# Nine moved channel blocks: statistics written from other queues, constant products put into TensorE's waits, and early mean shares made unscaled

## The reference

```python
def _displace(x, offset):            # 48 offsets, 8 channels each
    off_px = offset * 64.0
    off_int = round(off_px); sub = off_px - off_int
    # each block of 8 channels is shifted by (dx, dy) = off_int, zeros shifted in,
    # then convolved (3x3, same) with exp(-((kx+sub_x)^2 + (ky+sub_y)^2) / 0.5), normalised
    ...
x = x + _displace(_gn(x), offset)    # _gn: group norm, 32 groups of 12 channels
xr = transpose(_gn(x), (0, 2, 3, 1)).reshape(-1, 384)
y = pad(xr, 512) @ hadamard(512) / sqrt(512)
x = x + y[:, :384]                   # back in (16, 384, 32, 32)
```

## Time and profile before

| | us |
|---|---|
| median of 3 runs | 261.75 (259.67 to 261.84) |
| the profiled execution, device time | 261.49 |
| its span in the trace | 259.5 |
| what lies outside the span | 1.99 |

### The profile page before, as it was taken

One profiled execution on the slowest core, in us unless ns is written; L12 is line 12 of the kernel. 1 busy time (PEld: TensorE's weight loads), 2 busy tenths in 40 slices (PEclk: granted clock), 3 DMA queues, 4 the chain that ended last, 5 costly groups with the idle time before them and its releaser, 6 DMA issues.

```text
span 259.5 us, 2305 instructions
## 1 busy us (share of the span) xinstructions
PE 143.3 (55%) x616; PEld 87.5 (34%) x616; DVE 197.5 (76%) x321; ACT 136.2 (52%) x217; POOL 44.7 (17%) x49
## 2 busy tenths in 40 slices
PE   0000000508507249867920696999999999988610
PEld 0000000408507249756920532443333333333200
DVE  0799999999972169845760336999999999999940
ACT  1000999779761046035500199997788878880000
POOL 0000000000000053211233784000404184000000
PEclk9999999955955558997985559999999999999975
DMA  5999999999999208999960567219999999998798
GB/s 158 420 408 411 407 411 285 370 412 406 412 283 244 65 2 237 248 301 315 283 154 18 145 216 250 99 81 327 356 334 417 399 419 368 390 405 348 285 407 341
DMA packets 24845, 76.78 MB, mean 296 GB/s; under 512 B 6576, under 2 KB 6832, under 8 KB 24544
## 3 DMA queue, kind: packets, MB, share of 16 engines
q1 hardware_dynamic: 18928, 67.07, 71.7%
q0 software_dynamic: 5072, 9.51, 11.6%
q10 hardware_dynamic: 832, 0.05, 0.2%
HBM read 67.07 MB, written 29.99 MB: 374 GB/s over the span
## 4 chain that ended last, share of the span: by engine, by line
DVE 38%; DMA 33%; PE 9%; ACT 5%; issue 5%; SPq 5%; POOLq 0%; DVEq 0%
DMA ring<-x_pad 27%; DVE ring L934 22%; DVE parts L271 10%; PE ps L573 4%; PE ps L554 4%; DMA blk<-x_pad 4%; ACT blk L518 3%; DVE blk L271 2%; ACT parts L526 2%; DMA stat_rows<-blk_stat 2%; PE ps L563 2%; SPq L301 1%; SPq L289 1%; DVE halfstat L799 1%; DMA stat<-stat_rows 1%
## 5 line engine op out<-in xcount | busy, mean ns | idle before, releaser
L934 DVE SCALAR_TENSOR_TENSOR ring<-ps,beta,ring 128x1024 f32<-128x1024 f32 x48 | 59.8, 1280 | 0.0
L635 PE MATMUL ps<-parts,had_sb 128*128 128x512 f16 x216 | 54.0, 384 | 8.1 <-DVE parts L271 5.8
L563 PE MATMUL ps<-geo_sb,blk 128*128 128x128 f32 x72 | 12.5, 336 | 59.0 <-DMA blk<-x_pad 45.4
L799 DVE BATCH_NORM_STATS2 halfstat<-ring 128x6 f32<-128x512 f32 x64 | 38.9, 674 | 1.8 <-DMA ring<-x_pad 1.8
L573 PE MATMUL ps<-parts 128*128 128x160 f32 (+2 forms) x180 | 33.0, 348 | 10.4 <-ACT parts L460 10.4
L283 POOL DMA_INDIRECT ring<-x_rows,row_at x24 | 30.2, 1257 | 46.3 <-DMA ring<-x_pad 39.9
L518 ACT ACTIVATE blk<-ring,gn 128x1024 f32<-128x1024 f32 x32 | 37.8, 1226 | 0.0
L271 DVE TENSOR_TENSOR parts<-blk,parts 128x1024 f16<-128x1024 f32 x27 | 32.9, 1219 | 6.0 <-ACT parts L526 6.0
L573 PEld LDWEIGHTS ps<-parts 128*128 128x128 f32 x180 | 31.5, 225 | 11.4 <-ACT parts L460 10.6
L635 PEld LDWEIGHTS ps<-parts,had_sb 128*128 128x128 f16 x216 | 20.1, 99 | 44.0 <-DVE parts L271 13.2
L645 PE MATMUL ps<-ring,first_w 128*128 128x512 f32 x64 | 32.0, 624 | 0.0
(11 more groups left out here) (117 smaller groups left out, 136.6 us busy)
## 6 DMA issues: line engine op xcount, KB each, us to landing
ring<-x_pad SPq DMA_DIRECT2D x20, 1536.0 KB, 15.3
out<-ring SPq DMA_DIRECT2D x13, 1536.0 KB, 7.4
blk<-x_pad SPq DMA_DIRECT2D x15, 512.0 KB, 17.2
out<-ring SPq DMA_DIRECT2D x9, 512.0 KB, 6.0
x_rows<-blk POOLq DMA_DIRECT2D x6, 512.0 KB, 6.6
other_a<-x_pad SPq DMA_DIRECT2D x2, 512.0 KB, 9.1
x_rows<-other_a POOLq DMA_DIRECT2D x2, 512.0 KB, 6.5
geo_sb<-geo SPq DMA_DIRECT2D x1, 683.0 KB, 4.7
```

The lines of the kernel that those rows point to most:

```text
L563: last = pe.transpose(pixels[:, j // 4, 128 * (j % 4):128 * (j % 4 + 1)], shifted[:, 128 * j:128 * (j + 1)], eye)
L635: last = pe.matmul(ps[n % 4][:, h, :], had_sb[:, sign, :], part_of(n, t, part)[:, 512 * h:512 * (h + 1)], start=False, stop=ends and part ...
L799: last = dve.bn_stats(halfstat[:, i % 4, t, h, :], ring[:, t, place_of(i), 512 * h:512 * (h + 1)])
L934: dve.scalar_tensor_tensor(ring[:, m, place_of(i), :], ps[n % 4][:, :, :].rearrange("p a n -> p (a n)"), beta[:, i % BATCH:i % BATCH + 1], ...
```

## The change

- **Statistics of the blocks.** POOL no longer writes them. ACT does (`put_stat`), into a semaphore of its own, `stat_put`: blocks 0 to 3 inside its loop over the blocks, 4 to 8 behind its last mask. `blk_stat` has a slot for each block, so no buffer waits for the write. `blk_out` counts the write of the block only, 16. The read back of all statistics goes from POOL's queue to SP's, behind a wait for the nine writes.
- **Fetches of `blk_gn`.** SP issues those of blocks 0, 1, 3, 4 (before: 0, 1), ACT that of block 2 alone (before: 2, 3, 4).
- **Constant products.** `turn_over(n)` issues n products of the identity with 512 constant columns, into a PSUM half that nobody reads: 12 behind the early convolutions, 6 between the group sums and the first transposes of the block stage, 6 behind the last convolution.
- **Mean shares.** POOL makes the outer products of the unscaled `share`: block 0's as soon as DVE has made them (at image 8), block 1's behind ACT's last sum. To free `other_a` for this, ACT's two passes both write `aside[1]`, and the second waits for the first. When `blk_gn` is there, DVE works out one number for each block (`slope`, 128 x 1) and the addition is a SCALAR_TENSOR_TENSOR that scales the share.
- **DVE's order** at the start of the block stage: both partials, both additions, then mask 2, `finish(0)`, mask 3, `finish(1)`.

```diff
@@ sync
             def fetch_plain(k):
                 if k >= WIDE:
-                    sp.wait_ge(blk_out[k % WIDE], 32 * (k // WIDE))
+                    sp.wait_ge(blk_stat_done, k - WIDE + 1)
+                    sp.wait_ge(blk_out[k % WIDE], 16 * (k // WIDE))
...
-            for k in range(EARLY):
+            for k in (0, 1, 3, 4):
                 fetch_gn(sp, k)
...
+            sp.wait_ge(stat_put, 16 * FAST)
+            with sp.If(active > FAST):
+                sp.wait_ge(more_out, 32 * (OFFSETS - FAST))
+            sp.dma_start(stat[:, :, :, :].rearrange("p t b k -> p t (b k)"),
+                         stat_rows.rearrange("(t c) n -> c t n", t=CT)).then_inc(stat_patched, 16)
@@ gpsimd
             def leave(k, u):
-                c_at = pool.value_load(place[0:1, k, 0:1], min_val=0, max_val=CHANNELS - BIND)
                 pool.wait_ge(x1_done, k + 1)
                 pool.dma_start(x1_rows[...], own_x[u]).then_inc(blk_out[u], 16)
-                pool.wait_ge(blk_stat_done, k + 1)
-                pool.dma_start(stat_rows[...], blk_stat[:, u, :]).then_inc(blk_out[u], 16)
...
-                pool.wait_ge(slope_ready, k + 1)
+                pool.wait_ge(shares_made, 1)
+                if k == 1:
+                    pool.wait_ge(sum_stat_done, BATCH)
...
-            pool.dma_start(stat[...], stat_rows...).then_inc(stat_patched, 16)
@@ scalar
-                act.activation(aside[0], image, ACT.Identity, ..., accum_out=sums[:, 0, i:i + 1])
+                act.activation(aside[1], image, ACT.Identity, ..., accum_out=sums[:, 0, i:i + 1]).then_inc(sum_done_first, 1)
+                act.wait_ge(sum_done_first, i + 1)
...
-            for k in range(EARLY, DEEP + EARLY):
-                fetch_gn(act, k)
+            fetch_gn(act, EARLY)
+            def put_stat(k):
+                at = act.value_load(place[0:1, k, 0:1], min_val=0, max_val=CHANNELS - BIND)
+                act.wait_ge(blk_stat_done, k + 1)
+                act.dma_start(stat_rows[ds(at, BIND), :]..., blk_stat[:, k, :]).then_inc(stat_put, 16)
...
+                if k >= DEEP + EARLY:
+                    put_stat(k - DEEP - EARLY)
             mask_upper(FAST - 1)
+            for k in range(FAST - DEEP - EARLY, FAST):
+                put_stat(k)
@@ tensor
+            def turn_over(count):
+                for _ in range(count):
+                    pe.matmul(ps[1][:, 1, :], eye, geo_sb[:, G_SUM:G_SUM + 512], start=True, stop=True)
...
+            turn_over(12)
             group_sums(1, 0, lambda b: stat[:, b, :, 0])
             group_sums(2, 1, lambda b: moment[:, b, 1, :])
+            turn_over(6)
             pe.wait_ge(gn_done, 1)
...
+            turn_over(TURNS)
             group_sums(3, 0, ...)
@@ vector
             for k in range(EARLY):
                 dve.wait_ge(gn_in[k], 16)
-                dve.tensor_scalar(share[:, k, 0, :], share[:, k, 0, :], blk_gn[:, k, 0:1], blk_gn[:, k, 1:2],
-                                  ALU.mult, ALU.mult).then_inc(slope_ready, 1)
+                link(dve.tensor_tensor(slope[:, k:k + 1], blk_gn[:, k, 0:1], blk_gn[:, k, 1:2], ALU.mult))
                 partial(k).then_inc(partial_done, 1)
-            mask_block(EARLY)
             for k in range(EARLY):
                 dve.wait_ge(mean_share, k + 1)
                 dve.wait_ge(partial_done, k + 1)
-                dve.tensor_tensor(blk[:, k, :], blk[:, k, :], aside[k], ALU.add).then_inc(x1_done, 1)
+                dve.scalar_tensor_tensor(blk[:, k, :], aside[k], slope[:, k:k + 1], blk[:, k, :], ALU.mult, ALU.add).then_inc(x1_done, 1)
+            for k in range(EARLY):
+                mask_block(EARLY + k)
                 finish(k)
-                if k == 0:
-                    mask_block(EARLY + 1)
```

More of the change, by code:

```diff
@@ L32 @@
 EARLY_AT = 8
+TURNS = 6
 EARLY_FLIP = 10
@@ L158, in build @@
         blk_gn = sb("blk_gn", [128, FAST, 2])
+        slope = sb("slope", [128, EARLY])
         blk_half = sb("blk_half", [128, WIDE, 2, 6])
-        blk_stat = sb("blk_stat", [128, WIDE, 2])
+        blk_stat = sb("blk_stat", [128, FAST, 2])
         early = parts[:, :, :, :].rearrange("p a b c -> p (a b c)").bitcast(FP32)
@@ L209, in build @@
         centred = sem("centred")
-        slope_ready = sem("slope_ready")
+        shares_made = sem("shares_made")
         mean_share = sem("mean_share")
+        sum_done_first = sem("sum_done_first")
         partial_done = sem("partial_done")
@@ L233, in build @@
         stat_out = sem("stat_out")
+        stat_put = sem("stat_put")
         more_link = sem("more_link")
@@ L274, in fast_blocks_out @@
             for u in range(WIDE):
-                eng.wait_ge(blk_out[u], 32 * blocks_in(u))
+                eng.wait_ge(blk_out[u], 16 * blocks_in(u))
         def gather_part(eng, n, limit, signal):
@@ L347, in _ @@
                 for u in range(WIDE):
-                    sp.wait_ge(blk_out[u], 32 * blocks_in(u))
+                    sp.wait_ge(blk_out[u], 16 * blocks_in(u))
+                sp.wait_ge(stat_put, 16 * FAST)
                 with sp.Fori(FAST, OFFSETS) as k:
@@ L413, in _ @@
             pool.wait_ge(place_done, 1)
-            pool.wait_ge(stat_out, 16)
             for k in range(FAST):
@@ L449, in _ @@
                 act.activation(pivot[:, i:i + 1], image[:, 0:1], ACT.Copy)
-                act.activation(aside[0], image, ACT.Identity,
-                               bias=image[:, 0:1], scale=-1.0, accum_out=sums[:, 0, i:i + 1])
+                act.activation(aside[1], image, ACT.Identity,
+                               bias=image[:, 0:1], scale=-1.0, accum_out=sums[:, 0, i:i + 1]).then_inc(sum_done_first, 1)
+                act.wait_ge(sum_done_first, i + 1)
                 act.activation(aside[1], image, ACT.Square,
@@ L489, in _ @@
                     mask_upper(k - 1)
+                if k == DEEP + EARLY - 1:
+                    act.wait_ge(stat_out, 16)
+                if k >= DEEP + EARLY:
+                    put_stat(k - DEEP - EARLY)
             mask_upper(FAST - 1)
+            for k in range(FAST - DEEP - EARLY, FAST):
+                put_stat(k)
             active = act.value_load(count_i[0:1, 0:1], min_val=0, max_val=OFFSETS)
@@ L796, in _ @@
                     early_shares()
+                    dve.memset(scrap[:, 0:1], 0.0).then_inc(shares_made, 1)
                 for t in range(CT - 1):
@@ L884, in _ @@
                 dve.wait_ge(convolved, FAST)
+                dve.wait_ge(stat_put, 16 * FAST)
                 for u in range(WIDE):
-                    dve.wait_ge(blk_out[u], 32 * blocks_in(u))
+                    dve.wait_ge(blk_out[u], 16 * blocks_in(u))
                 with dve.Fori(FAST, OFFSETS) as k:
```

7 lines of the change are left out of this document (3 added, 4 removed).

## The result

| | before | after |
|---|---|---|
| median of 20 runs each | 262.56 (259.67 to 264.96) | 259.59 (256.45 to 262.11) |
| the profiled execution, device time | 261.49 | 259.88 |
| its span | 259.5 | 258.1 |

The ratio of after to before, run beside each other, is 0.986 with an interval of 0.983 to 0.989. That is 1.4% or 3.7 us faster. The ratio is taken over the fast runs of both kernels alone, those within 1.5% of the fastest, so it differs a little from that of the two medians, which are 3.0 us apart. The forecast was 254.1, in a range of 251.0 to 258.2. The sign is right, the gain is half of the 7.4 us forecast, and the time lies outside the range.

The account below looks back on a forecast made before the run. Bounds: DVE in the main stage; before it, slow-clock group sums with DVE's small steps, SP's DMA issue order, and the statistics' way. -5.0 (term 1 included) and -2.4 give -7.4 on 261.49: 254.1, range 251.0 to 258.2.

Parts of the forecast that it names:

- term 2: Block stage up to the last addition: earlier SP issues, shifted 7 at 102.6, last addition 5.0 us earlier, Term 1 included.
- about 105: Block stage: shifted 7's issue if two slow SP address loads come ahead and transposes stay slow, -3.3 us.
- rival (a): Block stage: DMA engines are the bound, earlier issues only land later; -3.9 us in all, 257.6; chance 0.20.
- The bound of the engines: Block stage: sixteen transfers at 296 GB/s take 28.3 us, through at 124.5, about when plain 8 lands at 124.8.
- Term 1: Group sums at the load stage's end: constant products keep the clock fast, second sum ends at 84.45 instead of 85.95, -1.5 us.
- My bound of -3.2: Group sums: the best case, if DVE isn't held and the clock is fast in both sums, -3.2 us.
- Term 3: Last block's statistics out and back: ACT writes, SP reads back, 5.5 us instead of 7.94, -2.4 us.
- Rival (c): After the last mask: ACT's last five issues are late through slow address loads, statistics' way +1.6 us, 258.1; chance 0.06.
- rival (d): Group sums: twelve constant products at the slow clock hold the first sum, +12.5 us; +6.6 in all, 268.1; chance 0.04.
- the cap by the gather: Main stage start: first gather lands at 139.9, doesn't bind, but caps further gain from the gn at 1.1 us.

Follow-up runs that it names:

- the kernel with `TURNS = 10` and late loads: Kernel after with SP's loads ahead, later POOL product, exchanged writes, block writes on ACT, ACT's loads before the `gn_rows` write, ten closing constant products: 0.977 against before.
- the later product: Kernel after with POOL's product for block 1 also waiting until DVE has handed over the sums (`sum_in`): 0.984 against before.
- the kernel with all edits together: Kernel after with SP's loads ahead, later POOL product, exchanged `gn_rows`/`stat_rows` writes, block writes on ACT, ACT's loads before the `gn_rows` write: 0.980 against before.
- the last kernel: Kernel after with SP's loads ahead, later product, exchanged writes, ACT's block writes, ACT's loads before its variance wait, ten closing constant products: 0.960 against before, median 251.27.
- the exchanged writes: Kernel after with SP's loads ahead, later POOL product, `gn_rows` written from ACT's queue and `stat_rows` from SP's: 0.971 against before, median 254.16.
- the last but one: Kernel after with SP's loads ahead, later product, exchanged writes, ACT's block writes, ACT's loads before its variance wait, six closing constant products: 0.961 against before, median 251.50.

## Why the forecast had the sign right and the size wrong

**The step that failed: term 2.** "Then one DMA each 1.3 us: ... shifted 7 at 102.6" and with it "-5.0 for the last addition". The trace gave +0.4, so the time gained came from terms 1 and 3 alone. What failed is that SP's issues were costed at 1.3 us each with every address load at its usual 0.28 us. I had seen one load of 1.91 us and allowed for two ahead of shifted 7 at the most, as a bound; two of them are 3.3 us, which from 102.6 gives 105.9 and not the "about 105" of that bound. There came three before it and two behind it, 7.4 us in all. The row I cited gave minimum, median and maximum of one line; the single loads of all three lines would have shown 4.5 us of excess before the change already. The rest of the working adds up: 102.6, and 1.0 for the first fetch (89.12 where I had 88.1), and 4.9 for the three slow loads ahead of shifted 7 make 108.5, and it went at 108.36. With the loads ahead of the stage it goes at 102.22, and the last addition comes 2.7 us earlier. But even then it begins at 129.06 and not 126.4. Landings had grown from 8.9 to 12.9 us, as rival (a) would have it. The bound of the engines that I had worked out "with no room to spare" from 296 GB/s allowed a last addition at 124.9, or 125.9 with the first fetch 1.0 us later than forecast, so at 295 GB/s it is not that bound which put it at 129.06. Only with the block writes on ACT's queue is the bound reached: 123.07 at 311 GB/s, with the first fetch 0.6 us earlier than forecast. So rival (a) is half right for a kernel whose SP keeps pace, and for the kernel after it isn't: its landings did not grow (8.9 us), and it lost the term to SP's loads.

That the block writes from POOL's queue slow the loads is shown by moving them to ACT: 7.4 to 2.3 us. What makes up the 2.3 us that remain, and by what path these writes act on SP, stays open.

**Term 1, -1.5 forecast, -0.5 measured.** The hold of DVE's TENSOR_SCALAR came as forecast from the one held row, 1.86 us for 0.17. The size is off in the second sum: forecast 1.6, measured 2.74. The hold that I counted as hidden behind the constant products ended 0.99 us after them, since they took 0.87 each and not 0.94. Over all kernels with twelve constant products the second sum goes with the idle time ahead of the first: without any it took 1.76, 1.78, 1.95, 2.06 and 2.29 us, with 0.99 it took 2.72, and with 1.8 to 2.5 it took 3.17, three times. One doesn't fit: the kernel with `TURNS = 10` and late loads had 0.46 us of idle time and 3.17. So the tendency is shown, a fixed relation isn't. By ratio the constant products are worth 0.7% or 1.8 us, which is near the 1.5 us of the term, though the term also holds the loss by POOL's product. My bound of -3.2 "if DVE isn't held and the clock is fast in both sums" is nearly what the later product gave: `gn` 2.5 us earlier than before, 84.6 for 87.1.

BN_STATS beside POOL's other product, for which I had taken 0, lost next to nothing. The product ran at 55.38 to 57.29, and DVE's four halves of an image took 2.47 us from 55.21 to 57.68, 2.42 elsewhere. Here the trace agrees with the Trainium skill (SBUF — State Buffer, "Who interferes with whom"), which says that a DVE instruction with at most one SBUF input, outside the two-port modes, does not contend with GpSimd. The held TENSOR_SCALAR of 1.86 us agrees with the same section, which counts tensor_scalar among the operations that can enter such a mode. It read SBUF; another TENSOR_SCALAR, which reads PSUM, took its usual 0.21 us beside POOL's product (at 80.02, product from 78.36 to 80.27, in the kernel with all edits together). Whether a TENSOR_TENSOR would be held too no run here shows: DVE's began when the product ended.

**Term 3, -2.4 forecast, -1.8 measured.** The statistics' write landed after 3.84 us, at the upper end of what I had allowed ("between 2.2 and 4.0"); a block write issued at 133.36 was still under way. The read back took 1.97 instead of 2.3. By ratio the statistics' part is worth 2.8 us, give or take 1. If more than the 1.8 is in it, that may lie in the plain fetches that wait for one write less; no run separates that.

**The rest.** Rival (c), ACT's late issues, did not come: the other issues were done when the last statistics came at 134.64, and theirs went out at 134.80. The address loads of `put_stat` took up to 1.16 us, less than the 1.9 feared. Nor did rival (d): the constant products ran fast, 0.87 us each. The third sum stayed at 3.19 us as forecast. The main stage passed on what its start gained (1.4 us at ACT's start, 1.6 us at the end), and the cap by the gather, worked out as a further 1.1 us, showed itself in the last kernel as a wait of 2.27 us. The raw shares and DVE's new order were credited with 0.5 us on the mask of block 2 (95.8 for 96.30). It began at 96.62, and alone this part measures nothing.

## What to carry to other kernels

Read every address that a DMA issue needs before the stage that is bound by its issues; a load that takes 0.28 us at the median can take 2 in the place where it matters, and the sum of all its lines, not one line's median, is its price. Constant products paid here where little idle time followed them, and not for the second sum where 1.8 us or more did, so look first at what else can hold the step behind them. When a sequencer's pace is bettered, ask what the landings do then: here half of the gain was taken back by longer ones, and it came with the large writes on another queue. A full share of the DMA engines does not say that they are the limit.

## What the runs showed of the hardware

- SP's loads of an address, 0.28 us at the median, took 1.1 to 2.0 us five times in the block stage, four of them within 1.5 us behind a block write's issue on POOL. With these writes on ACT's queue the longest was 1.30. Nine loads in a row on ACT, none of them slow, delayed a write by some 4 us.
- Shares of 1.00, 0.99 and 0.98 of the DMA engines went with 270, 299 and 311 GB/s from 97 to 125 in three kernels that move the same blocks (after, the exchanged writes, the last but one). In these traces the share does not tell what the engines could move.
- With block writes on POOL's queue the load of plain block 6, issued at 106.29, let its addition begin at 120.03; with them on ACT's queue, issued at 106.00, at 116.46.
- Beside a POOL product of 1.91 us a DVE TENSOR_SCALAR that reads SBUF took 1.86 us instead of 0.17, one that reads PSUM its usual 0.21.
- From the issue of `gn`'s write to the first fetch it took 1.9 us when issued at 87.20 on SP's queue, and 3.2 when issued at 84.31 on ACT's: part of what an earlier `gn` brings is lost on the way out. The cause was not separated.
